# A tokenizer fed with host-laid patches in two halves of the batch, its global scores taken through the weights, and expert weights laid out by the host

## The chip, the cores and the metric

The kernel runs on one core of a Trainium2 chip. The metric is the device time of one execution in microseconds (us); the number compared is the median of several executions. One more execution is recorded by the hardware profiler, and all rows below come from it.

A core has five engines with an instruction stream each: TensorE (PE, matrix products into PSUM), VectorE (DVE), ScalarE (ACT), GpSimd (POOL) and SyncE (SP), which here issues nearly all loads and stores. They meet through semaphores. Transfers run on 16 DMA engines, whose mean busy share is the "DMA" of the profile.

## The reference, cut to what matters

A batch of 64 images and 77 text tokens of width C = 256 each go through three stages.

```python
# tokenizer: patches of 14x14x3 = 588 pixels, 6x6 of them used, as 2x2 windows of 3x3 patches
pe  = conv(x, conv_w, stride=14)
red = mean of pe over each window                       # (64, 4, C)
q   = ln(red) @ la_wq ; k, v = ln(window) @ la_wkv      # 1 query, 9 keys per window, 8 heads of 32
local_out = red + softmax(q k / 16) v @ la_proj_w + la_proj_b
gq  = ln(class_emb) @ ga_wq ; gk, gv = ln(local_out) @ ga_wkv   # 1 query, 4 keys per image
cls_out   = class_emb + softmax(gq gk / 16) gv @ ga_proj_w + ga_proj_b
patch_out = local_out @ mod_w + mod_b
h = concat([patch_out (4), cls_out (1), txt (77)])      # T = 82 tokens per image
# attention, 16 heads of 16, with a relative bias per head
h = h + softmax(q k * scale + bias) v @ w_out + b_out
# experts of low rank: 8 of them, two per token, for the first tokens of the list
h = h + sum over 2 experts of w_e * gelu(ln(h) @ w1A_e.T @ w1B_e) @ w2A_e.T @ w2B_e
```

The convolution has one set of weights for all patches. `gq` is the same for all images, because `class_emb` is.

## The kernel before

The program is three functions, one block each, with a barrier between them: `tokenizer_block` (from L55), `attention_block` (L637) and `expert_block` (L1080). The batch of 64 x 82 = 5248 tokens is 41 tiles of 128 rows. They stand in SBUF as `h_flat`; the tokenizer writes its five tokens per image to a list in memory (`fused_rows`), into which one long transfer (L148) has put the text, and the whole list is read back into `h_flat`.

**Tokenizer.** It works in 18 tiles of 128 patches: 64 images by the two windows `wi` of a column, for each `wj`, and for each of nine places (r, c) in the window. For a tile VectorE copies the pixels together (`copy_patch`, L404), TensorE turns them in five transposes (L253), ScalarE copies those to SBUF (L357, L359), and TensorE multiplies them with the turned convolution weights in five chunks, four of 128 pixels and one of 76 (`conv`, L227). VectorE copies the product (L499) and takes its statistics (L501). Then come 21 projections: the class query, and for each half `wj` one query and nine times keys and values, 512 wide. For each, VectorE normalises (`normalise`, L517), TensorE turns the rows (`xnT`, L269) and multiplies (`project`, L278), VectorE reads the product with a bias row (`consume`, L522). These loops are written out by hand and hold the order on each engine: on VectorE the normalise of item n stands ahead of the read of item n - 2. The gains of the layer norms are multiplied into the weights beforehand (L466), their offsets go through the weights as "shift rows" (L217). Window attention is VectorE's: products (L542), their sums (L545), softmax (L549 to L555), weighting (L558), sum over the keys (L562). The tails on TensorE: turn (L308), output projection (L317), patch output (L325), global keys and values (L335), turn and class projection (L340, L344). POOL takes the reciprocal roots (L185, L187) and scatters the slots of the experts' lists in 32 indirect transfers (L177).

**What SP's queue sets.** All loads are issued on SP in the order of the program: routing tables, identity, convolution weights, six transfers of images (L138), weights (L142), bias rows, the text (L148); after the last convolution `wqkv` (L150), after the patch outputs their four stores (L156), after the class token its store (L158), and when these have landed the four loads of `h_flat` (L162).

**Attention and experts.** At the start of its block SP issues `wout` (L709), the bias row, five tables (L712) and the expert weights (L713 to L716), then the stores of finished tiles (L721). VectorE's first instruction that needs the tables is at L1041. The expert block turns the first factors `w1a` and `w2a` with TensorE (L1186, L1192) and ScalarE copies (L1273, L1277), while the tokens of the first slots are gathered (L1143) and their statistics taken (L1335).

Of the kernel before, what the change touches and what calls it, by code (L numbers as in the profile page):

```python
# [14 lines left out]
C = 256  # L15
# [14 lines left out]
CHUNKS = [128, 128, 128, 128, PIX - 512]  # L30
# [14 lines left out]
def col(ap, n):  # L45

    return ap.rearrange("(c p) -> p c", p=128)


# [5 lines left out]
def tokenizer_block(nc, S, I, R, H, ident_all):  # L55

    NN = NTOK // 128 * TOPK
    with ExitStack() as ctx:
# [3 lines left out]
        img = sb("img", [128, CS, CIN, PS, IMG])  # L66

        early = R["early"]
        cw_nat = early[:, 0:2 * PIX].rearrange("p (t x) -> p t x", t=2)
        cwT = early[:, 2 * PIX:2 * PIX + 5 * C].rearrange("p (q c) -> p q c", q=5)  # L70
        patch = early[:, 2 * PIX + 5 * C:4 * PIX + 5 * C].rearrange("p (u x) -> p u x", u=2)
        patchT = early[:, 4 * PIX + 5 * C:].rearrange("p (u q t) -> p u q t", u=2, q=5)
        attn = R["attn"]
        wraw = attn["wraw"]
        pe = sb("pe", [128, WIN, NW, C])

        spare = img[:].rearrange("p r c y x -> p (r c y x)")
        kv = spare[:, 0:WIN * NW * 2 * C].rearrange("p (w n c) -> p w n c", w=WIN, n=NW)
        prod = spare[:, WIN * NW * 2 * C:WIN * NW * 2 * C + NW * C].rearrange("p (n c) -> p n c", n=NW)
        red = sb("red", [128, WIN, C])  # L80
        xn = sb("xn", [128, 2, C])
        xT = sb("xT", [128, 2, 2, 128])
        qv = sb("qv", [128, WIN, C])
# [3 lines left out]
        vec = sb("vec", [128, 8, 2])  # L87
        shiftb = sb("shiftb", [128, 4, 2, 128])
        bq_row = sb("bq_row", [128, C]); bkv_row = sb("bkv_row", [128, 2 * C])
        gbq_row = sb("gbq_row", [64, C]); gbkv_row = sb("gbkv_row", [64, 2 * C])  # L90
        pj_row = sb("pj_row", [128, C]); mod_row = sb("mod_row", [128, C]); gpj_row = sb("gpj_row", [64, C])
        cls = sb("cls", [64, C])
        NS = 20
        stats = sb("stats", [128, NS + 3, 6]); mv = sb("mv", [128, NS + 3, 2]); rs = sb("rs", [128, NS + 3])
        mhalf = sb("mhalf", [128, NS + 3])
        sc = sb("sc", [128, NW, H8]); sx = sb("sx", [128, H8]); ssum = sb("ssum", [128, H8]); rsum = sb("rsum", [128, H8])
        agg = sb("agg", [128, WIN, C]); aggT = sb("aggT", [128, 2, 2, 128])
# [25 lines left out]
        def _(sp):  # L123
# [29 lines left out]
            for wi in range(WIN):  # L153
                for wj in range(WIN):
                    t = wi * WIN + wj
                    sp.dma_start(fused[:, t, :], pout[64 * wi:64 * wi + 64, wj, :]).then_inc(S["tok_out"], 16)  # L156
# [1362 lines left out]
```

## Time and profile before

| | |
|---|---|
| median of three executions | 851.23 us (851.07 to 852.0) |
| the profiled execution | 855.09 us, span 853.3 us, 21494 instructions |
| TensorE busy | 688.8 us (81%), weight loads 529.1 us (62%) |
| VectorE, ScalarE, POOL busy | 551.9 us (65%), 394.6 us (46%), 287.4 us (34%) |
| mean granted clock of TensorE | 0.905 |

The time of an execution is the span plus what lies around it. TensorE's granted clock is written as a share of full speed: 1.00 is 2.4 GHz, 0.50 is 1.2 GHz. In a row of the timeline, the first number is the start in us from the span's start, the second the duration; then engine, line, operation, out<-in, the tile and how many instructions the row takes together; in brackets is how long the engine had stood idle and what released it. "SPq" is SP's queue of DMA issues; such a row tells of the issue, not of the transfer.

### The profile page before, as it was taken

The numbers are of one execution on the slowest core, as the hardware profiler recorded it, in microseconds if no ns is written. First come the engines' busy times: TensorE is split into PE (matmuls) and PEld (weight loads), VectorE is DVE, ScalarE is ACT, GpSimd is POOL, SyncE is SP. The second block draws the span as 40 slices with busy tenths as digits, with TensorE's granted clock in tenths as the row PEclk, the third lists the DMA queues.
The fourth block names the chain that finished last, engine by engine and source line by source line (L and its number), as shares of the span: only waits on it lengthen the run. The fifth ranks groups of instructions, "written<-read, shape, count | busy, mean of one in ns | idle before, by whom it ended". The sixth has DMA issues, their size and how long they took to land. (4 is left out here: it accounts for less than half of the span.)

```text
span 853.3 us, 21494 instructions
## 1 busy us (share of the span) xinstructions
PE 688.8 (81%) x8366; PEld 529.1 (62%) x8366; DVE 551.9 (65%) x1189; ACT 394.6 (46%) x931; POOL 287.4 (34%) x361
## 2 busy tenths in 40 slices
PE   1869696471469999999999999999987479999960
PEld 1657542320247777777778777777775468888850
DVE  0536658834448888888888888788772246666625
ACT  1111111000035676666666666667664335555533
POOL 2375200001282333334143323340001455767333
PEclk9979899775669999999999999999997679999985
DMA  8990100004920000000000000000000412222127
GB/s 153 218 324 12 37 1 0 1 12 152 317 39 8 15 15 15 15 18 17 14 15 15 14 15 15 15 21 14 15 15 19 99 58 68 82 70 75 52 72 268
DMA packets 34691, 51.20 MB, mean 60 GB/s; under 512 B 8960, under 2 KB 26208, under 8 KB 34464
## 3 DMA queue, kind: packets, MB, share of 16 engines
q1 hardware_dynamic: 29440, 39.55, 16.4%
q0 software_dynamic: 5152, 10.29, 4.2%
q8 instruction: 68, 1.11, 0.6%
q14 instruction: 31, 0.25, 0.1%
HBM read 36.89 MB, written 18.00 MB: 64 GB/s over the span
## 5 line engine op out<-in xcount | busy, mean ns | idle before, releaser
L1023 DVE TENSOR_REDUCE mx<-psS 82x8 f32<-82x656 f32 x128 | 106.3, 831 | 34.1 <-PE psS L825 34.1
L834 PE MATMUL psP<-ident_all,prob 82*82 82x82 f32 x1024 | 118.7, 239 | 9.3 <-ACT probT L960 9.3
L960 ACT ACTIVATE probT<-psP 82x328 f32<-82x328 f32 x256 | 112.4, 439 | 27.3 <-PE psP L834 27.3
L834 PEld LDWEIGHTS psP<-ident_all,prob 82*82 82x82 f32 x1024 | 91.1, 121 | 53.6 <-issue 30.1
L755 POOL TENSOR_TENSOR h_flat<-h_flat,po 128x256 f32<-128x256 f32 x41 | 29.8, 726 | 257.0 <-ACT po L947 257.0
L1025 DVE TENSOR_TENSOR prob<-psS,mx 82x656 f32<-82x656 f32 x128 | 107.0, 836 | 4.4
L952 ACT ACTIVATE prob<-prob 82x656 f32<-82x656 f32 x128 | 94.3, 738 | 0.0
L802 PE MATMUL psQ<-hT,early 128*128 128x328 f32 x256 | 85.5, 459 | 0.6 <-ACT hT L915 0.5
L812 PE MATMUL psQ<-early,hT 128*82 128x256 f32 x256 | 67.4, 387 | 0.1
L930 ACT ACTIVATE oT<-psO 128x328 f32<-128x328 f32 x64 | 28.4, 443 | 75.9 <-PE psO L846 75.9
L825 PE MATMUL psS<-kT,qT 32*82 32x82 f32 x2048 | 53.9, 243 | 10.4 <-DVE kT L1011 10.4
L825 PEld LDWEIGHTS psS<-kT,qT 32*82 32x82 f32 x2048 | 44.1, 150 | 18.2 <-DVE kT L1011 12.8
L802 PEld LDWEIGHTS psQ<-hT,early 128*128 128x128 f32 x256 | 44.9, 195 | 13.5 <-issue 1.9
L1295 ACT ACTIVATE f_hT<-psH 128x1024 f32<-128x1024 f32 x39 | 39.9, 1024 | 27.1 <-PE psH L1224 26.4
L742 POOL TENSOR_SCALAR xh<-h_flat,a_mv,a_rst 128x256 f32<-128x256 f32 x41 | 50.2, 1224 | 4.5
L846 PE MATMUL psO<-probT,vv 82*32 82x82 f32 x2048 | 50.1, 239 | 1.3 <-ACT attT L939 1.3
L1157 POOL DMA_INDIRECT entry_rows<-yv,slot_entry x39 | 39.9, 1022 | 29.0 <-ACT yv L1302 22.2
L1011 DVE SCALAR_TENSOR_TENSOR qT<-psQ,ownq,qadd 128x328 f32<-128x328 f32 x64 | 32.8, 555 | 25.4 <-PE psQ L802 25.3
L1224 PE MATMUL psH<-t1T,w1bs 64*128 64x128 f32 x624 | 47.6, 294 | 0.0
L227 PE MATMUL tk_ps<-early 128*128 128x256 f32 (+1 forms) x180 | 47.1, 415 | 0.0
L1236 PE MATMUL psT<-f_hT,w2as 128*64 128x128 f32 x624 | 43.5, 282 | 4.2 <-DVE t L1377 4.2
L1011 DVE SCALAR_TENSOR_TENSOR kT<-psQ,own,kadd 128x328 f32<-128x328 f32 x64 | 32.8, 555 | 20.3 <-PE psQ L802 20.3
(222 smaller groups left out, 1300.7 us busy)
## 6 DMA issues: line engine op xcount, KB each, us to landing
img<-in_x SPq DMA_DIRECT2D x6, 1008.0 KB, 20.6
out<-h_flat SPq DMA_DIRECT2D x41, 128.0 KB, 1.7
fused_rows<-in_txt SPq DMA_DIRECT2D x1, 4928.0 KB, 25.1
h_flat<-entry_rows SPq DMA_DIRECT2D x6, 512.0 KB, 6.3
h_flat<-fused_rows SPq DMA_DIRECT2D x1, 2176.0 KB, 16.6
ex_w2a<-in_ff_w_A SPq DMA_DIRECT2D x1, 2048.0 KB, 12.3
ex_w1b<-in_ff_w_B SPq DMA_DIRECT2D x2, 1024.0 KB, 17.2
out<-h_flat SPq DMA_DIRECT2D x8, 256.0 KB, 4.5
```

What stands on the lines that cost most here:

```text
L742: pool.tensor_scalar(xh[:, n % 3, :], H[:, n, :], mv[:, n % 4, 0:1], rst[:, n % 4:n % 4 + 1], ALU.subtract, ALU.mult).then_inc(S["xh_ready ...
L802: mm = te.matmul(bank(("qk", 4 * q + j))[:, 0:QT], wqkv[:, c, 128 * j:128 * j + 128], hT[:, c, a:a + QT], start=(c == 0), stop=(c == 1))
L812: mm = te.matmul(bank(("val", b))[0:T, 0:C], hT[:, c, a:a + T], wv[:, c, :], start=(c == 0), stop=(c == 1))
L825: mm = te.matmul(psS[0:T, g, s:s + T], qT[rows, par, a, t, cols], kT[rows, par, a, t, cols], start=True, stop=True)
L834: mm = te.transpose(psP[0:T, s * T:s * T + T], prob[:, b % 2, g, s, :], ident_all[0:T, 0:T])
L846: mm = te.matmul(psO[32 * k:32 * k + 32, s * T:s * T + T], vv[:, b % 4, h, :], probT[:, b % 2, h % 8 // 2, 2 * (h // 8) + h % 2, :], start ...
L952: act.activation(prob[:, b % 2, 2 * half:2 * half + 2, :, :], prob[:, b % 2, 2 * half:2 * half + 2, :, :], ACT.Exp).then_inc(S["prob_ready ...
L960: act.activation(probT[:, b % 2, g, :, :].rearrange("p s t -> p (s t)"), psP[0:T, 0:4 * T], ACT.Copy).then_inc(S["probT_ready"], 1)
L1011: ins = v.scalar_tensor_tensor(out=dst[:, q % 2, a, t, :].rearrange("p (b t) -> p b t", b=4), in0=bank(("qk", 4 * q + j))[:, 0:QT].rearran ...
L1023: v.tensor_reduce(mx[:, half, :, :], s4, X, ALU.max).then_inc(S["max_ready"], 1)
L1025: v.tensor_tensor(prob[:, b % 2, 2 * half:2 * half + 2, :, :], s4, mx[:, half, :, :].unsqueeze(3).to_broadcast([T, 2, 4, T]), ALU.subtract ...
L1224: mm = te.matmul(psH[:, j % 2, half, f * 128:f * 128 + 128], w1bs[rows, j % 2, f * 128:f * 128 + 128], t1T[rows, j % 2, :], start=True, st ...
```

## The change

- **Patches.** The host lays `x` out as `patches` (for each of 18 tiles, five chunks of 118 pixels by 128 columns, the last two rows of zeros) and the convolution weights as `conv_rows`. `PCH` is 118. `copy_patch`, the transposes and their copies go; patches come in five groups of 1, 3, 5, 4 and 5 tiles (`GROUPS`), issued between the other loads.
- **Two halves.** A tile now holds the four windows of 32 images. Tiles 0 to 8 are the first half, 9 to 17 the second. `items` is the order of the 22 projections. The second half's convolutions stand on TensorE behind the first half's projections, the first half's tail between them, and its tokens are stored, and the tiles 0 to 19 of `h_flat` loaded, ahead of the second half's.
- **Order.** On VectorE `consume(n)` now stands ahead of `normalise(n + 2)`, and the dot products are taken per key (`dots`), behind both. Values are read by ScalarE, the sum over the window, the residual and the list scatters (15 and 17) are POOL's. The shift rows of the global weights stand on TensorE behind projection 6.
- **Global scores through the weights.** The scores come from `wgs`, the global key weights times the class query, summed by head, so the global keys are not computed. The weighted values of the four windows are added by a product with the matrix `sel`.
- **Hand-over.** Tiles 20 to 40 of `h_flat` are loaded at the start of the attention block, once the second half's tokens have landed, ahead of its constants.
- **Experts.** `w1a` and `w2a` come turned from the host; their transposes and copies go, and a buffer `yg_hi` of its own holds what shared one. The rest of attention and experts is as before.

The diff, cut ("..." stands for what is left out):

```diff
+PCH = -(-PIX // 5)
+H_LOADS = ((0, 3), (3, 20), (20, 30), (30, 41))
...
+        items += [("kv", h, 0), ("kv", h, 1), ("q", h, 0)]
+        if h == 1:
+            items.append(("lg", 0, 0))
+        items += [("kv", h, k) for k in range(2, NW)]
+        if h == 0:
+            items.append(("gq", 0, 0))
+    items.append(("lg", 1, 0))
+    place = {item: n for n, item in enumerate(items)}
+    mv_order = [("gq", 0, 0)] + [("kv", 0, k) for k in range(NW)] + [("q", 0, 0)] + [("kv", 1, k) for k in range(NW - 1)]
...
+        patches = big[0:PCH, 0:18 * 5 * 128].rearrange("p (n q t) -> p n q t", n=18, q=5)
+        H = big[:, 0:NB * T // 128 * C].rearrange("p (n c) -> p n c", c=C)
+        cwT = sb("cwT", [PCH, 5, C])
...
-            sp.dma_start(cw_nat, I["conv_w"].rearrange("(t p) c y x -> p t (c y x)", p=128)).then_inc(S["conv_in"], 16)
-            for r in range(CS):
-                for wi in range(WIN):
-                    y0 = (wi * CS + r) * PS
-                    sp.dma_start(img[64 * wi:64 * wi + 64, r, :, :, :],
-                                 I["x"][:, :, y0:y0 + PS, :]).then_inc(S["img_in%d" % r], 16)
-            for name, tile in (("la_wq", wq), ("la_wkv", wkv), ("la_proj_w", wpj), ("ga_wq", gwq), ("ga_wkv", gwkv),
-                               ("ga_proj_w", gwpj), ("mod_w", wmod)):
-                sp.dma_start(tile[:], I[name].rearrange("(c p) n -> p c n", p=128)).then_inc(S["tk_w_in"], 16)
...
+            sp.dma_start(cwT[:], I["conv_rows"]).then_inc(S["conv_in"], 16)
+            for k, (lo, hi) in enumerate(GROUPS):
+                if k == 1:
+                    sp.dma_start(ident_all[:], I["ident"]).then_inc(S["ident_in"], 16)
+                    sp.dma_start(cols[:], I["cols"]).then_inc(S["ident_in"], 16)
+                    sp.dma_start(cls[:], row(I["class_emb"], 128)).then_inc(S["ident_in"], 16)
+                    sp.dma_start(entry[:], I["entry"]).then_inc(S["r_entry"], 16)
+                    sp.dma_start(R["list"], I["unfilled"]).then_inc(S["r_entry"], 16)
+                if k == 3:
+                    sp.dma_start(wq[:], I["la_wq"].rearrange("(c p) n -> p c n", p=128)).then_inc(S["law_in"], 16)
+                    sp.dma_start(wkv[:], I["la_wkv"].rearrange("(c p) n -> p c n", p=128)).then_inc(S["law_in"], 16)
+                sp.dma_start(patches[:, lo:hi, :, :], I["patches"][:, lo:hi, :, :]).then_inc(S["img_in%d" % k], 16)
+            sp.dma_start(gwq[:], I["ga_wq"].rearrange("(c p) n -> p c n", p=128)).then_inc(S["gaw_in"], 16)
+            sp.dma_start(gwkv[:], I["ga_wkv"].rearrange("(c p) n -> p c n", p=128)).then_inc(S["gaw_in"], 16)
+            for name, tile in (("la_proj_w", wpj), ("mod_w", wmod), ("ga_proj_w", gwpj)):
+                sp.dma_start(tile[:], I[name].rearrange("(c p) n -> p c n", p=128)).then_inc(S["prw_in"], 16)
...
+                for w in range(HW):
+                    sp.dma_start(fused[HB * h:HB * h + HB, w, :], pout[HB * w:HB * w + HB, h, :]).then_inc(S["tok_out%d" % h], 16)
+                sp.wait_ge(S["cout_ready"], h + 1)
+                sp.dma_start(fused[HB * h:HB * h + HB, HW, :], cout[:, h, :]).then_inc(S["tok_out%d" % h], 16)
+                if h == 0:
+                    sp.wait_ge(S["txt_in"], 16)
+                    sp.wait_ge(S["conv_done"], 18)
+                    sp.wait_ge(S["tok_out0"], 16 * 5)
+                    for k, (lo, hi) in enumerate(H_LOADS[:2]):
+                        sp.dma_start(H[:, lo:hi, :], R["fused"][128 * lo:128 * hi, :].rearrange("(n p) c -> p n c", p=128)).then_inc(S["h_in%d" % k], 16)
...
+            rstd(0)
+            for k in range(1, NW):
+                add_patch(0, k)
+                if k % 3 == 2:
+                    rstd(1 + k // 3)
...
+            pool.wait_ge(S["r_entry"], 32)
             pool.wait_ge(S["r_addr"], 1)
-            for n in range(NN):
-                pool.indirect_dma_start(out=slots, out_offset=bass.IndirectOffsetOnAxis(addri[:, n:n + 1], 0),
-                                        in_=entry[:, n:n + 1], in_offset=None).then_inc(S["r_listed"], 16)
+            list_entries(0, 15)
+            residual(0)
+            for k in range(1, NW):
+                add_patch(1, k)
+                if k == 2:
+                    rstd(5)
+                if k == 5:
+                    rstd(6)
+            rstd(7)
+            rstd(8)
+            rstd(9)
+            residual(1)
+            list_entries(15, NN)
...
-                te.wait_ge(S["patchT_ready"], 2 * (n + 1))
                 if n == 0:
-                    te.wait_ge(S["cwT_ready"], 5)
+                    te.wait_ge(S["conv_in"], 16)
+                for k, (lo, hi) in enumerate(GROUPS):
+                    if n == lo:
...
+                if n == 9:
+                    te.wait_ge(S["v_read"], NW)
+                for q in range(5):
+                    mm = te.matmul(PS8[n % 2][:, 0:C], patches[:, n, q, :], cwT[:, q, :], start=(q == 0), stop=(q == 4))
                 mm.then_inc(S["conv_done"], 1)
...
+            for n in range(6):
+                conv(n)
...
+            shift_rows(0, wq, slice(0, C), PS8[4][:, 0:C])
+            shift_rows(1, wkv, slice(0, 2 * C), PS8[5][:, :]).then_inc(S["shift_ps"], 1)
+            for n in range(6, 9):
+                conv(n)
+            xnT(0)
+            for n in range(10):
+                if n < 9:
+                    xnT(n + 1)
+                project(n)
+                if n == 6:
+                    te.wait_ge(S["gaw_in"], 32)
+                    te.wait_ge(S["shiftb_ready"], 4)
+                    te.wait_ge(S["shift_rows"], 2)
+                    shift_rows(2, gwq, slice(0, C), PS8[4][:, 0:C])
+                    shift_rows(3, gwkv, slice(C, 2 * C), PS8[4][:, C:2 * C]).then_inc(S["shift_ps"], 1)
+            for n in range(9, 16):
+                conv(n)
...
+            project(10)
+            conv(17)
+            xnT(11)
+            turn_lout(0)
...
+            def normalise(n):
+                kind, h, k = items[n]
...
+                v.tensor_scalar(xn[:, n % 2, :], src, mv[:, m, 0:1], rs[:, m:m + 1], ALU.subtract, ALU.mult).then_inc(S["xn_ready"], 1)
+            def consume(n):
+                kind, h, k = items[n]
...
+                v.wait_ge(S["proj_ps"], n + 1)
+                if kind == "kv":
+                    v.tensor_tensor(kv[:, k, 0:C], bank[:, 0:C], bkv_row[:, 0:C], ALU.add).then_inc(S["proj_read"], 1)
...
+            def dots(k):
+                chain(v.tensor_tensor(kv[:, k, 0:C], kv[:, k, 0:C], qv[:], ALU.mult))
+                chain(v.tensor_reduce(sc[:, k, :], kv[:, k, 0:C].rearrange("p (h d) -> p h d", h=H8), X, ALU.add))
...
+            for n in range(10):
+                consume(n)
+                if n + 2 < 10:
+                    normalise(n + 2)
+                if n >= 3:
+                    dots(n - 3)
+                if n == 8:
+                    v.wait_ge(S["shift_ps"], 2)
+                    v.tensor_copy(gbq_row[:], PS8[4][:, 0:C]).then_inc(S["shift_rows"], 1)
+                    v.tensor_copy(gbv_row[:], PS8[4][:, C:2 * C]).then_inc(S["shift_rows"], 1)
...
+            sp.wait_ge(S["tok_out1"], 16 * 5)
+            for k, (lo, hi) in list(enumerate(H_LOADS))[2:]:
+                sp.dma_start(H[:, lo:hi, :], A["fused"][128 * lo:128 * hi, :].rearrange("(n p) c -> p n c", p=128)).then_inc(S["h_in%d" % k], 16)
...
+def patch_rows(x):
+    s = CS * PS
+    a = np.asarray(x)[:, :, :WIN * s, :WIN * s].reshape(2, NB // 2, CIN, WIN, CS, PS, WIN, CS, PS)
+    a = a.transpose(2, 5, 8, 0, 4, 7, 3, 6, 1).reshape(PIX, 2 * NW, 128)
+    a = np.concatenate([a, np.zeros((5 * PCH - PIX, 2 * NW, 128), a.dtype)])
+    return a.reshape(5, PCH, 2 * NW, 128).transpose(1, 2, 0, 3)
```

SP's queue of loads before, from the tables on (names are out<-in with the shape):

```order
L131 DMA entry<-in_entry 128x32
L132 DMA slot_list<-in_unfilled 16x384
L133 DMA ident_all<-in_ident 128x128
L134 DMA early<-in_conv_w 128x2x588
L138 DMA img<-in_x 64x3x1344 x6
L142 DMA wq<-in_la_wq 128x2x256
L142 DMA wkv<-in_la_wkv 128x2x512
L142 DMA wpj<-in_la_proj_w 128x2x256
L142 DMA gwq<-in_ga_wq 128x2x256
L142 DMA gwkv<-in_ga_wkv 128x2x512
```

The same queue now (`big` is the tile that `patches` and `h_flat` share):

```order
L139 DMA cwT<-in_conv_rows 118x1280
L150 DMA big<-in_patches 118x640
L142 DMA ident_all<-in_ident 128x128
L143 DMA cols<-in_cols 128x26
L144 DMA cls<-in_class_emb 128x256
L145 DMA entry<-in_entry 128x32
L146 DMA slot_list<-in_unfilled 16x384
L150 DMA big<-in_patches 118x1920
L150 DMA big<-in_patches 118x3200
L148 DMA wq<-in_la_wq 128x2x256
L149 DMA wkv<-in_la_wkv 128x2x512
L150 DMA big<-in_patches 118x2560
```

Six image transfers into 64 partitions have become five into 118, with the weights between them; a last patch group and the global weights follow.

TensorE before, around the shift rows of the global keys and values (`tk_ps` is PSUM, `early` the turned patches and the convolution weights):

```order
L227 MATMUL tk_ps<-early 128x256 x5
L217 MATMUL tk_ps<-gwkv,shiftb 64x512 x2
L253 MATMUL tk_ps<-ident_all,early 128x128 x4
L253 MATMUL tk_ps<-ident_all,early 76x128
L227 MATMUL tk_ps<-early 128x256 x5
```

TensorE now, from projection 6 of the first half to its last:

```order
L289 MATMUL tk_ps<-wkv,xT 128x256 x2
L297 MATMUL tk_ps<-wkv,xT 128x256 x2
L257 MATMUL tk_ps<-gwq,shiftb 128x256 x2
L257 MATMUL tk_ps<-gwkv,shiftb 128x256 x2
L268 MATMUL tk_ps<-ident_all,xn 128x128 x2
L289 MATMUL tk_ps<-wkv,xT 128x256 x2
L297 MATMUL tk_ps<-wkv,xT 128x256 x2
L268 MATMUL tk_ps<-ident_all,xn 128x128 x2
L289 MATMUL tk_ps<-wkv,xT 128x256 x2
L297 MATMUL tk_ps<-wkv,xT 128x256 x2
```

The global shift rows have moved from between the convolutions to between the projections, and the convolutions L251 of the second half stand behind them.

VectorE before, in the projections of the first half (`img` holds the keys and values):

```order
L517 TENSOR_SCALAR xn<-pe,mv,rs 128x256
L522 TENSOR_TENSOR img<-tk_ps,bkv_row 128x512
L517 TENSOR_SCALAR xn<-pe,mv,rs 128x256
L522 TENSOR_TENSOR img<-tk_ps,bkv_row 128x512
L517 TENSOR_SCALAR xn<-pe,mv,rs 128x256
L522 TENSOR_TENSOR img<-tk_ps,bkv_row 128x512
```

VectorE now, in the same place:

```order
L611 TENSOR_TENSOR kv<-tk_ps,bkv_row 128x256
L603 TENSOR_SCALAR xn<-pe,mv,rs 128x256
L626 TENSOR_TENSOR kv<-kv,qv 128x256
L627 TENSOR_REDUCE sc<-kv 128x8
L611 TENSOR_TENSOR kv<-tk_ps,bkv_row 128x256
L603 TENSOR_SCALAR xn<-pe,mv,rs 128x256
```

The read of the keys has moved ahead of the next normalise, and the dot product of an earlier key follows both.

## Rows read from the trace of the kernel before

**Rows 1.** Waits of SP's queue: waited for, total, times, longest (us).
```profile
SPq L156 <- DVE pout L615: 82.0, 1, 82.0
SPq L150 <- PE tk_ps L227: 52.0, 1, 52.0
SPq L158 <- DVE pe L630: 20.5, 1, 20.5
```

**Rows 2.** Timeline, the hand-over to attention.
```profile
200.98 0.45 SPq L158 DMA_DIRECT2D fused_rows<-pe  x1
202.90 6.04 SPq L162 DMA_DIRECT2D h_flat<-fused_rows  x4
...
223.38 0.17 DVE L1041 TENSOR_SCALAR ownq<-own 128x2 f32<-128x2 f32 x1 [10.08 <-DMA own<-in_own]
...
241.61 1.43 PE L825 MATMUL psS<-kT,qT 32*82 32x82 f32 x32
```

**Rows 3.** Page, part 6, DMA issues: KB each, us from issue to landing.
```profile
img<-in_x SPq DMA_DIRECT2D x6, 1008.0 KB, 20.6
```

**Rows 4.** Windows: stretch, length, busy of PE, PEld, DVE, ACT, POOL, clock, DMA share, GB/s.
```profile
25.00:30.00 5.00, 4.45 (x13) 3.11 (x11) 4.47 (x13) 0.97 (x4) 0.00 (x0) 1.00 1.02 210
210.00:215.00 5.00, 0.00 (x0) 0.00 (x0) 3.20 (x7) 0.00 (x0) 3.78 (x6) 0.50 1.10 350
```

**Rows 5.** Timeline of the first 60 us: an SP issue, a list scatter, two convolutions' time.
```profile
5.25 0.44 SPq L131 DMA_DIRECT2D entry<-in_entry  x1
...
34.91 0.97 POOL L177 DMA_INDIRECT slot_list<-entry,addri  x1 [0.30 <-issue]
...
44.99 2.33 PE L227 MATMUL tk_ps<-early 128*128 128x256 f32 x10
...
55.52 4.33 PE L227 MATMUL tk_ps<-early 128*128 128x256 f32 x10
```

**Rows 6.** Timeline, window attention of the second half on VectorE.
```profile
157.15 2.55 DVE L545 TENSOR_REDUCE sc<-img 128x72 f32<-128x2304 f32 x1
...
161.67 2.56 DVE L558 TENSOR_TENSOR img<-img,sc 128x2304 f32<-128x2304 f32 x1
...
164.26 4.02 DVE L562 TENSOR_REDUCE agg<-img 128x256 f32<-128x2304 f32 x1
```

**Rows 7.** Timeline, projections and what VectorE does between them.
```profile
107.70 1.88 PE L278 MATMUL tk_ps<-wkv,xT 128*128 128x512 f32 x4
...
109.64 1.88 PE L278 MATMUL tk_ps<-wkv,xT 128*128 128x512 f32 x4
...
125.73 0.41 DVE L517 TENSOR_SCALAR xn<-pe,mv,rs 128x256 f32<-128x256 f32 x1
...
126.19 0.44 PE L269 MATMUL tk_ps<-ident_all,xn 128*128 128x128 f32 x2
126.20 0.42 DVE L522 TENSOR_TENSOR qv<-tk_ps,bq_row 128x256 f32<-128x256 f32 x1
```

**Rows 8.** Timeline, the tails: turn, POOL's roots, softmax, class projection.
```profile
168.34 0.69 PE L308 MATMUL tk_ps<-ident_all,agg 128*128 128x128 f32 x2 [10.09 <-DVE agg L562]
...
173.81 0.71 POOL L187 TENSOR_TENSOR rs<-rs,mhalf 128x2 f32<-128x2 f32 x1
...
192.46 0.17 DVE L549 TENSOR_SCALAR sc<-sc 64x32 f32<-64x32 f32 x1
...
197.24 0.47 PE L340 MATMUL tk_ps<-ident_all,pe 64*128 64x64 f32 x2 [8.10 <-DVE pe L562]
...
200.53 0.42 DVE L630 TENSOR_TENSOR pe<-pe,gpj_row 64x256 f32<-64x256 f32 x1
```

**Rows 9.** Timeline, the start of the expert block.
```profile
671.09 1.09 ACT L1277 ACTIVATE w2aT<-psH 128x512 f32<-128x512 f32 x2 [0.25 <-PE psH L1192]
...
674.21 1.40 DVE L1335 BATCH_NORM_STATS2 f_stats<-xin 128x6 f32<-128x256 f32 x4 [17.42 <-DMA xin<-out,slot_token]
```

**Rows 10.** Page, first line.
```profile
span 853.3 us, 21494 instructions
```

More of the change, by code:

```diff
@@ L116, in tokenizer_block, with gain, shift, stat_of @@
         slots = R["list"].rearrange("p j -> (p j)").rearrange("(n a) -> n a", a=1)
-        tiles = [(wj, r, c) for wj in range(WIN) for r in range(CS) for c in range(CS)]
+        fused = R["fused"].rearrange("(b t) c -> b t c", t=T)
+        def gain(k, c):
+            return cols[:, 4 * k + c:4 * k + c + 1]
+        def shift(k):
+            return cols[:, 4 * k + 2:4 * k + 4]
+        def stat_of(item):
+            kind, h, k = item
+            return {"kv": 10 * h + 1 + k, "q": 10 * h, "lg": 20 + h, "gq": 22}[kind]
         block = ctx.enter_context(nc.Block())
@@ new lines, in project @@
+                if kind == "kv":
+                    h = items[n][1]
+                    before = [m for m in range(n % 2, n, 2) if items[m][0] == "kv" and items[m][1] == h]
+                    if before:
+                        te.wait_ge(S["v_read"], v_count[items[before[-1]]])
+                    te.wait_ge(S["pe_ready"], 9 * h + 9)
+                    for c in range(2):
+                        mm = te.matmul(PS8[n % 2][:, 0:C], xT[:, n % 2, c, :], w[:, c, C:2 * C], start=(c == 0), stop=(c == 1))
@@ new lines, in _ @@
+            copy_pe(9)
+            copy_pe(10)
+            exponent(0)
+            for n in range(11, 16):
+                copy_pe(n)
+            copy_aggT(0)
+            copy_xT(10)
+            copy_pe(16)
+            copy_pe(17)
+            copy_xT(11)
+            copy_loutT(0)
+            for n in range(11, 22):
+                if n < 21:
+                    copy_xT(n + 1)
+                copy_v(n)
+                if n == 14:
+                    act.wait_ge(S["bias_ps"], 1)
+                    for c in range(2):
+                        ins = act.activation(wqkv[:, c, :], wqkv[:, c, :], ACT.Copy, scale=cols[:, 16 + c:17 + c])
+                    ins.then_inc(S["wqkv_scaled"], 1)
+                if n == 15:
+                    global_exponent(0)
+                if n == 19:
+                    copy_gaggT(0)
@@ L622, in _, with statistics @@
[L622 to L630 removed]
+            def statistics(item, src):
+                k = stat_of(item)
+                chain(v.bn_stats(stats[:, k, :], src))
+                v.bn_aggr(mv[:, k, :], stats[:, k, :]).then_inc(S["mv_ready"], 1)
@@ new lines, in _ @@
+            v.wait_ge(S["shift_rows"], 2)
+            normalise(0)
+            normalise(1)
+            mean_patch(0)
+            for n in range(10):
+                consume(n)
[7 more added lines that the diff above has]
+                    v.tensor_copy(gbv_row[:], PS8[4][:, C:2 * C]).then_inc(S["shift_rows"], 1)
```

820 lines of the change are left out of this document (403 added, 417 removed).

## The prediction, made before the changed kernel had run

> **What bounds the kernel now.** I read the waits of the DMA queue first, then the timeline of the first 250 us, then busy time by windows. The program runs as three blocks with a barrier between them: tokenizer, attention, experts. The diff rewrites the first, hands attention its inputs differently, and drops one preparation from the third. SP's queue shows the skeleton of the tokenizer [rows 1]: 52.0 us until the last convolution, 82.0 until the patch tokens, 20.5 until the class token. It is one chain with nothing beside it: images, convolutions, projections, window attention, residual, patch token, class attention; the last DMA of tokens goes out at 200.98, all hidden rows are read back from 202.90 on, and attention's first real work waits until 223.38 for constants queued behind that read-back; the first scores start at 241.61 [rows 2]. Attention from there on is the same code, so I carry it over unchanged: the change is worth what it moves the moment of 223.38.
>
> **What a load costs.** The images come as six transfers into 64 partitions each [rows 3] and run with all engines busy at 210 GB/s; the read-back into 128 partitions runs at 350 [rows 4]. Divided by 16 engines that is 13.1 and 21.9 GB/s each, and into 64 partitions 26.3 GB/s for every eight of them. The Trainium skill (SBUF — State Buffer, the section on the DMA port swizzle) says that 64 partitions reach 8 of the 16 ports, at some 27 GB/s a port; the trace's 210 against 350 agrees.
>
> The new loads have 118 rows: the 588 pixels of a patch as five chunks of 118 instead of four of 128 and one of 76. All transfers of this trace have a first dimension that 16 divides (64, 128 or 16 rows), so it shows only even splits over 16 engines. If the split has to be even, 118 = 2 x 59 leaves two engines. That is my forecast's assumption, and I give it most of the chance because every transfer here, read by its GB/s, is shared evenly. The Trainium skill says it outright (DMA: Bandwidth & Descriptors, "Why a DMA increments its semaphore by 16 and not by 1"): the number of engines is the largest one up to 16 that divides the slowest dimension of both sides, 100 partitions giving 10 and 127 giving 1. No run here shows an uneven case, and by that rule the forecast stands.
>
> Each of the two engines then moves 59 rows of 5,120 bytes of convolution weights and 18 patches x 2,560 bytes: 59 x 51,200 = 3.02 MB. All other loads use all engines and queue behind on these two; up to the global query and key weights that adds a sixteenth of 1.5 MB, with small things 0.12 MB, so 3.14 MB each. The sixth issue of SP's queue begins at 5.25 [rows 5], data flow from about 7 and the last receipt takes 1. How fast one engine goes alone no row shows. From below: 21.9 GB/s, what each gets when 16 share the memory (13.1 as the extreme, the image rate). I take 26.3, the rate per eight partitions, as an engine that writes row after row should find no wider door than such a group. So the global weights land at t: 3.14 MB / 26.3 GB/s = 119 us after the start at 8, t = 127 us (at 21.9 GB/s: 151). The skill's page on DMA gives 27 GiB/s per engine; by that, an estimate, t would be 116.
>
> **Where that bites.** TensorE runs the first half of the batch (convolutions 0 to 8, then ten projections). Its sixth to ninth patch arrives with the third group, (0.302 MB of weights + 0.151 + 0.453 + 0.755 of patches)/26.3 = 63 us of transfer, so at about 71; three and more convolutions at 2.33 (4.33 at half clock) [rows 5], shift rows and seven projections take it to 71 + 16 + 22 = 109. Then it stands before the shift rows of the global weights, in order, until 127: projections 7 to 9, the second half's convolutions and all the rest are queued behind. Both patch groups of the second half have landed by then.
>
> **From t to the class token.** Five pieces, with durations of before:
> 1. Four shift matmuls at half clock, 4.33 / 5 = 0.87 each: 3.5, and three projections of 3.06 (piece 3): 12.7.
> 2. Nine convolutions x 2.33 = 21, with the transposes, output projection and class query between them 2.5: 23.5. VectorE's softmax and sums of the first half (2.56 + 4.02 and small ones) [rows 6] lie beside.
> 3. Eleven projections. Before, one began every 1.94 (107.70, 109.64): the next normalise was issued ahead of the read of the last projection. Now it stands behind it on VectorE, and TensorE's next transposes wait for it: 1.88 of matmuls + 0.27 from the transposes' start to the next projection's, + read 0.42 + normalise 0.41 [rows 7], and 0.08 for the handovers = 3.06. Nine of these are 27.5; query and global item 3.3; patch output and the 14 bias matmuls 3.8: 34.6. The dot products, 0.9 each, now fit in VectorE's gaps instead of 2.56 for the products and 2.55 for their sums at the end.
> 4. Last read, two dot products, softmax, weighting 2.56, sum 4.02, shift row 0.42: 11.3.
> 5. The global tail, at half clock as before [rows 8]: from the turn at 168.34 to the rstd on POOL, done at 174.52, 6.2; normalise 0.4; the patch output and transposes ahead of it on TensorE 2.5; projection with scores 2.6; softmax as 192.46 to 194.02, 1.6; weighting on a fourth of the numbers 0.6; class projection from its turn at 197.24 to the last sum at 200.95, 3.7: 17.6.
> Sum 99.7, say 100, so the class token is ready at 227 (before at 200.95).
>
> **Hand-over.** Only tiles 20 to 40 are still to be read: 2.75 MB with 0.65 MB of constants behind it. Before it was 5.25 + 0.65 MB in 20.5 us (202.90 to 223.38) [rows 2], of which 16.9 at 350 GB/s; now 9.7 + 3.6 = 13.3, and 2.6 until the last store has landed: 16 where it was 22.4. The constants arrive at 243, against 223.4: **+20 us**.
>
> **What I cost at nothing.** POOL's 32 list scatters (0.97 and 0.30 between them, so 1.27) [rows 5] move, 15 behind the first half's patch sums and 17 behind the second mean; both lie in TensorE's stretches, 22 us against some 45 to the next thing asked of POOL. Without that cover the last rstd would be late by what is left. Patch copies, transposes (five per patch) and their ACT copies go, 18 x 0.6 us of TensorE; they would count were TensorE not waiting for data. Expert weights: eight turns end at 672.2, but VectorE starts at 674.21 on the gathered tokens [rows 9], so their removal gains nothing; 0.5 MB more is loaded beside attention.
>
> The sum is made against the profiled execution, 855.09 us (span 853.3) [rows 10]; the median of the runs is 851.23, 3.9 lower. A difference carries over, so 851.2 + 20 = **871 us**.
>
> **The rivals.**
> *The 118 rows are spread over all engines.* For it: loads of both widths kept all 16 engines busy, and nothing in the trace refuses an uneven split. Then 6.04 MB need 17 us at 350 GB/s, TensorE is never short of data: index matmuls to 11, six convolutions to 27, shift rows, three more to 36, seven projections of 3.06 to 60. From there 100 less 3 for a warm clock, and 16: 173 instead of 223.4, so 801 us. Its chance is 0.17.
> *One engine alone is faster than eight partitions' share.* At 29 GB/s t is 116 and the time 860; at 32 and above the constants arrive no later than 223.4 and nothing is lost. It decides the sign from 32 GB/s on. Chance 0.06; against it, the fastest stretch read here gives an engine 21.9 [rows 4].
> *An engine alone gets its image rate, 13.1 GB/s,* because latency per row and not the port is its limit: t = 248, the time 992. Chance 0.02: in the read-back an engine does 21.9 with rows of 1 KB.
>
> **How the numbers follow.** Forecast (two engines at 21.9 to 28 GB/s) 0.75. Its own range is 864 to 895; with 7 us of doubt on the five pieces, 857 to 902. Taken down to 846, for the second rival, the range leaves out the first and the third and little else, 0.2 in all. 0.2%, 1.7 us, is what a measurement can tell. Faster by more: the first rival whole, half the second and a little of the forecast, 0.22. Within: 0.03. Slower: 0.75.
>
> **What would show it.** In the profile after: the DMA share in the first 120 us near 2/16 instead of full, GB/s near 50; time to landing of the patch groups 20 to 40 us each; TensorE idle of some 18 us at the shift rows of the global weights, released by a DMA; projection spacing 3.1; class token 100 after that; a_w constants 16 later. It is wrong if the DMA share is full for the first 20 us (then 801), or if the projections run at 2 us, which would give back up to 10, or if attention's batches take another time than now.

## The result, and the profile after

The changed kernel takes 877.62 us (median of 4, 876.2 to 878.3), the kernel before 851.62: 26 us slower. The ratio on record is 1.0289 (95% interval 1.0264 to 1.0314); the two medians divide to 1.0305, inside that interval. Forecast were 871 us, 20 slower, with a range of 846 to 902.

The page of the changed kernel, its span, granted clock, DMA share and GB/s in 40 slices:

```profile
span 876.5 us, 21431 instructions
PEclk9767969977567999999999999999998579999995
DMA  2111327003290000000000000000000312222117
GB/s 56 62 74 54 101 89 255 8 1 122 71 319 15 8 14 15 21 14 14 15 20 14 15 15 20 15 14 14 15 21 13 84 56 73 68 89 73 48 58 278
```

A slice is 21.9 us. For the first 130 us the DMA share is one to three tenths, where images before ran on all engines [rows 4]. A stretch in which only patches move, TensorE standing still, by windows (columns as in [rows 4]):

```profile
60.00:70.00 10.00, 0.00 (x0) 0.00 (x0) 0.00 (x0) 0.00 (x0) 0.00 (x0) 0.50 0.12 52
```

0.12 of 16 engines is two, and 52 GB/s are 26 each. The trace also holds every update of the semaphore that a transfer counts up as it lands. The third patch group gives three: one at 23.3, as soon as it is issued, and two as its data lands, at 72.2 and 72.9. The two loads of global weights have 128 rows and give 32: 28 of them between 93.1 and 101.9, the last four between 127.5 and 131.0. So 14 engines had delivered their part of these weights 29 us before the two that were still busy with patches.

TensorE's longest waits (waited for, total, times, longest):

```profile
PE tk_ps L251 <- DMA big<-in_patches: 49.4, 3, 19.4
PE tk_ps L257 <- DMA gwkv<-in_ga_wkv: 19.9, 1, 19.9
PE psX L1334 <- DVE f_xn L1470: 17.4, 2, 16.3
PE tk_ps L268 <- DVE xn L603: 16.5, 16, 1.5
PE psO L920 <- DMA own<-in_own: 14.8, 1, 14.8
```

Patches are waited for three times, then the global weights, once, for 19.9 us. The wait for `xn` now stands behind nearly every read, 16 times; in the kernel before, TensorE waited for `xn` six times, 14.3 us together, 6.9 of it the first time. The timeline, in the order of the prediction's steps (the row of SP is the issue of `gwq`, described at the end):

```profile
71.35 19.78 SPq L151 DMA_DIRECT2D gwq<-in_ga_wq  x1
72.98 6.54 PE L251 MATMUL tk_ps<-cwT,big 118*128 118x256 f32 x20 [19.44 <-DMA big<-in_patches]
...
131.08 2.08 PE L257 MATMUL tk_ps<-gwq,shiftb 128*128 128x256 f32 x4 [19.92 <-DMA gwkv<-in_ga_wkv]
...
142.43 15.35 PE L251 MATMUL tk_ps<-cwT,big 118*128 118x256 f32 x70 [0.56 <-ACT kv L444]
...
165.80 0.44 PE L268 MATMUL tk_ps<-ident_all,xn 128*128 128x128 f32 x2 [1.10 <-DVE xn L603]
...
172.01 2.84 PE L399 MATMUL tk_ps<-cols,wqkv 128*128 128x1 f32 x24
...
203.34 1.03 PE L297 MATMUL tk_ps<-wkv,xT 128*128 128x256 f32 x4
...
215.78 0.69 PE L308 MATMUL tk_ps<-ident_all,agg 128*128 128x128 f32 x2 [11.41 <-DVE agg L649]
...
233.69 0.41 DVE L680 TENSOR_TENSOR cout<-tk_ps,cls_row 32x256 f32<-32x256 f32 x1 [3.38 <-PE tk_ps L352]
234.13 0.30 SPq L166 DMA_DIRECT2D fused_rows<-cout  x1
...
248.33 0.17 DVE L1186 TENSOR_SCALAR ownq<-own 128x2 f32<-128x2 f32 x1 [9.84 <-DMA own<-in_own]
...
268.94 1.42 PE L970 MATMUL psS<-kT,qT 32*82 32x82 f32 x32
...
697.57 1.41 DVE L1458 BATCH_NORM_STATS2 f_stats<-xin 128x6 f32<-128x256 f32 x4 [16.32 <-DMA xin<-out,slot_token]
```

The constants arrive at 248.33 instead of 223.38 [rows 2], 25.0 later; the experts start at 697.57 instead of 674.21 [rows 9], 23.4 later; the span ends 23.2 later. The loss arises before attention. The medians differ by 26.0, more than the spans, because the profiled execution of before (855.09) lies 3.5 above the median of its runs and that of after (878.3) only 0.7.

### The profile page after: what moved, and what is told of

It reads as the page before. It is cut to its first block and busy times, and to the rows that moved or that the text cites. A ratio compares the mean times of both kernels' runs of the same rounds, so it can differ in the third digit from the quotient of the medians.

```text
span 876.5 us, 21431 instructions
## 1 busy us (share of the span) xinstructions
PE 667.2 (76%) x8314; PEld 526.6 (60%) x8314; DVE 526.5 (60%) x1182; ACT 391.6 (45%) x926; POOL 296.0 (34%) x382
## 5 line engine op out<-in xcount | busy, mean ns | idle before, releaser
L900 POOL TENSOR_TENSOR big<-big,po 128x256 f32<-128x256 f32 x41 | 29.8, 726 | 257.0 <-ACT po L1092 257.0
L947 PE MATMUL psQ<-hT,wqkv 128*128 128x328 f32 x256 | 86.8, 465 | 0.5 <-ACT hT L1060 0.5
L251 PE MATMUL tk_ps<-cwT,big 118*128 118x256 f32 x180 | 46.6, 422 | 50.0 <-DMA big<-in_patches 49.4
L251 PEld LDWEIGHTS tk_ps<-cwT,big 118*128 118x128 f32 x180 | 38.2, 215 | 58.5 <-DMA big<-in_patches 34.3
L957 PE MATMUL psQ<-wqkv,hT 128*82 128x256 f32 x256 | 66.7, 383 | 0.1
L970 PEld LDWEIGHTS psS<-kT,qT 32*82 32x82 f32 x2048 | 43.8, 149 | 18.3 <-DVE kT L1156 12.8
L947 PEld LDWEIGHTS psQ<-hT,wqkv 128*128 128x128 f32 x256 | 45.9, 199 | 14.1 <-issue 2.8
L887 POOL TENSOR_SCALAR xh<-big,a_mv,a_rst 128x256 f32<-128x256 f32 x41 | 50.2, 1224 | 4.5
L427 ACT ACTIVATE pe<-tk_ps 128x256 f32<-128x256 f32 x18 | 6.9, 383 | 97.4 <-PE tk_ps L251 97.4
## 6 DMA issues: line engine op xcount, KB each, us to landing
ex_w2aT<-in_w2aT SPq DMA_DIRECT2D x1, 2048.0 KB, 12.4
```

The costliest lines, as they stand in the source:

```text
L251: mm = te.matmul(PS8[n % 2][:, 0:C], patches[:, n, q, :], cwT[:, q, :], start=(q == 0), stop=(q == 4))
L887: pool.tensor_scalar(xh[:, n % 3, :], H[:, n, :], mv[:, n % 4, 0:1], rst[:, n % 4:n % 4 + 1], ALU.subtract, ALU.mult).then_inc(S["xh_ready ...
L947: mm = te.matmul(bank(("qk", 4 * q + j))[:, 0:QT], wqkv[:, c, 128 * j:128 * j + 128], hT[:, c, a:a + QT], start=(c == 0), stop=(c == 1))
L957: mm = te.matmul(bank(("val", b))[0:T, 0:C], hT[:, c, a:a + T], wv[:, c, :], start=(c == 0), stop=(c == 1))
L970: mm = te.matmul(psS[0:T, g, s:s + T], qT[rows, par, a, t, cols], kT[rows, par, a, t, cols], start=True, stop=True)
```

## The experiments

The engines of a transfer, first. One edit, four numbers; each adds rows of zeros to the patches and the convolution weights, with the same instructions:

```diff
-PCH = -(-PIX // 5)
+PCH = 128          # also 120, 124, 127
```

> The changed kernel with 128 rows in place of 118 for patches and convolution weights (the rest zeros, 6.55 MB instead of 6.04). My theory (a transfer is shared only by as many engines, up to 16, as divide its rows): all 16 engines work, the patches land within about 20 us, TensorE finds no data missing, the constants of attention arrive near 175 us instead of 248.3, the time is 800 to 806 us. Rival (the slow loading comes from something else, as the form of the source in memory or loads that stand between the patches): the DMA share stays near 2/16 and the time at 870 to 885 us.

> 120 rows. My theory (largest divisor up to 16): 15 engines, DMA share near 0.9 while the patches load, time 800 to 807 us as with 128 rows. Rival (only multiples of 16, or powers of two, are spread; all else goes on 2 engines): near 877 us.

> 124 rows = 4 x 31. My theory: 4 engines, DMA share 4/16, some 104 GB/s; each moves 1.71 MB until the global weights have landed, at about 8 + 65 = 73 us, as TensorE finishes its seventh projection near 77; the time is then 820 to 830 us. Rival (2 engines for all that 16 does not divide): near 877 us. Rival (rows shared out unevenly, the slow 118 having another cause): near 803.

> 127 rows, a prime. My theory: one engine, DMA share 1/16, 26 GB/s; it moves 6.6 MB until the global weights have landed at about 8 + 252 = 260 us, 129 us later than with 118 rows; the time is near 1006 us. If one engine alone is faster than each of two were together (29 GB/s), 980 us. Rival (2 engines): near 885.

These four ran on a chip on which the kernel before took 902.2 us (median of 7), so differences and ratios count, not the times. On it TensorE also stood before transposes of `xn` (L268) without a releaser ("issue", 11.4 us in the tokenizer with 128 rows, 6.9 with 120, 5.6 with 127); neither the changed kernel's trace nor that of 128 rows on another chip shows it.

| rows | engines by the divisor | time | ratio to before | moved to the 851.6 of the other chips |
|---|---|---|---|---|
| 128 | 16 | 849.5 us | 0.9411 (0.9348 to 0.9475) | 801 us |
| 120 | 15 | 850.4 us | 0.943, one execution | 803 us |
| 124 | 4 | 876.9 us | 0.972, one execution | 828 us |
| 118 | 2 | 877.6 us | 1.0289, another chip | 877.6 us |
| 127 | 1 | 1045.1 us | 1.158, one execution | 986 us |

Windows of the four kernels in the same stretches; with 128 rows and with 120:

```profile
20.00:30.00 10.00, 10.00 (x44) 8.04 (x44) 3.18 (x12) 2.40 (x7) 5.99 (x10) 1.00 1.02 396
```

```profile
20.00:30.00 10.00, 9.33 (x44) 7.89 (x43) 2.90 (x11) 1.74 (x5) 4.41 (x8) 1.00 1.01 241
```

With 124 and with 127:

```profile
60.00:70.00 10.00, 7.41 (x29) 5.24 (x28) 4.04 (x12) 1.86 (x5) 6.03 (x9) 0.79 0.25 98
```

```profile
60.00:70.00 10.00, 0.00 (x0) 0.00 (x0) 0.00 (x0) 0.00 (x0) 0.00 (x0) 0.50 0.06 26
```

0.25 is four engines and 0.06 one; 98 and 26 GB/s are 24.5 and 26 each. With 120 rows the share is 1.01 where 0.9 was expected, so it doesn't tell 15 engines from 16. The updates of the semaphore do. The third patch group has one early update and then as many as engines deliver: 2 with 118 rows, 15 with 120, 4 with 124, 1 with 127; with 128 rows all 16 come together (17.2 to 19.3 us).

The order of the times is that of the largest divisor and not of the bytes: 127 rows are fewer than 128 and cost 196 us more. That shows the forecast's assumption. The rivals of two engines for every count that 16 does not divide fall with 120 and 124. The time of 127 rows, moved by the ratio, is 986 and lies nearer to the 980 of a faster lone engine than to 1006, but the ratio also shrinks a wait for data, and one engine moves 26 GB/s on this chip as each of two does on the other. In the trace the global weights release TensorE at 261.37, where 260 was expected, 130 after the 131.08 of 118 rows. From there to attention's constants (389.62) it is 128.3 us, 11 more than the 117.3 of 118 rows, which I put down to the slower chip. The constants were expected near 175 with 128 rows; on this chip they came at 189.90.

The same 118 rows without padding, in two transfers (the waits for them count to 32 in place of 16), and 128 rows once more:

```diff
-            sp.dma_start(cwT[:], I["conv_rows"]).then_inc(S["conv_in"], 16)
+            for a, b in ((0, 112), (112, PCH)):
+                sp.dma_start(cwT[a:b, :, :], I["conv_rows"][a:b, :, :]).then_inc(S["conv_in"], 16)
...
+                for a, b in ((0, 112), (112, PCH)):
+                    sp.dma_start(patches[a:b, lo:hi, :, :], I["patches"][a:b, lo:hi, :, :]).then_inc(S["img_in%d" % k], 16)
```

> The changed kernel with its 118 rows, each of its six transfers cut in two, of rows 0 to 111 and 112 to 117. My theory (112 = 16 x 7, so all 16 engines; 6 rows go on 6): DMA share full in the first 20 us, the same time as with 128 rows within 3 us, a ratio of 0.938 to 0.944. Rival (it is the 118 in the tile, its 5,120 and 2,560 byte rows or its place in memory, and not the rows of one transfer): the ratio stays at 1.029.

> The kernel of 128 rows once more, beside split112 and on a chip that is not the first one if it falls so. By the first ratio, 0.941, and the time of the kernel before: 801 us where the kernel before takes 851. If the first chip's idle of TensorE between instructions in the tokenizer was part of the ratio, a ratio of 0.935 to 0.94.

split112: 806.93 us, ratio 0.9455 (0.9418 to 0.9491). rows128_again: 804.53 us, 0.9448 (0.9405 to 0.9491); the kernel before took 852.76 beside both. The tile, its rows and its data are those of the changed kernel, and 71 us go with the cut alone: it is the number of rows of one transfer. Its semaphores agree: the pair of transfers of the third patch group gives 23 updates, 16 for 112 rows and 1 + 6 for the six. With 128 rows the constants come at 170.07 on this chip (175 expected). The ratio of 128 rows is somewhat above the first one, within its interval, and not at the 0.935 to 0.94 that were expected if the first chip's idle was part of it.

Then the order of the loads in the starved queue, with 118 rows:

```diff
                 if k == 3:
                     sp.dma_start(wq[:], ...)
                     sp.dma_start(wkv[:], ...)
+                    sp.dma_start(gwq[:], I["ga_wq"].rearrange("(c p) n -> p c n", p=128)).then_inc(S["gaw_in"], 16)
+                    sp.dma_start(gwkv[:], I["ga_wkv"].rearrange("(c p) n -> p c n", p=128)).then_inc(S["gaw_in"], 16)
                 sp.dma_start(patches[:, lo:hi, :, :], I["patches"][:, lo:hi, :, :]).then_inc(S["img_in%d" % k], 16)
-            sp.dma_start(gwq[:], I["ga_wq"].rearrange("(c p) n -> p c n", p=128)).then_inc(S["gaw_in"], 16)
-            sp.dma_start(gwkv[:], I["ga_wkv"].rearrange("(c p) n -> p c n", p=128)).then_inc(S["gaw_in"], 16)
```

> The changed kernel with 118 rows, its two loads of global weights moved ahead of the two patch groups of the second half. My theory (TensorE stands at the shift rows of the global weights for 19.9 us because they queue behind patches that it needs only later): they land near 76 us, the wait goes, the second half's convolutions begin 18 us earlier, at 124 instead of 142, with their patches there by then; 18 us less than the changed kernel, a ratio near 1.009. Rival (the starved queue only shows up as a wait for the last patches): the ratio stays at 1.02 to 1.03.

862.25 us, ratio 1.0103 (1.0082 to 1.0123) beside a kernel before of 852.61, against 1.0289: some 16 us of the 26 come back (15.4 by the medians), where 18 were expected. TensorE's waits have lost that for `gwkv`, and hold the three for patches as before:

```profile
PE tk_ps L251 <- DMA big<-in_patches: 50.4, 3, 20.8
```

The second half's convolutions begin at 125.28 (124 expected), and attention's constants come 16.9 us earlier than in the changed kernel:

```profile
231.47 0.17 DVE L1186 TENSOR_SCALAR ownq<-own 128x2 f32<-128x2 f32 x1 [10.00 <-DMA own<-in_own]
```

This shows the step "where that bites": the 19.9 us of waiting at the global shift rows were on the path.

Then VectorE's order in the projections, with 128 rows:

```diff
-                consume(n)
                 if n + 2 < 10:
                     normalise(n + 2)
+                consume(n)
```

(and the same in the second half's loop).

> The kernel of 128 rows, with VectorE's normalise(n + 2) ahead of consume(n) again in both projection loops. My theory (TensorE waits for the normalise behind the read, 3.2 us from projection to projection): the spacing falls to about 1.95, some 16 to 18 projections gain 1.2 each, 20 us less than with 128 rows alone, a ratio to the kernel before near 0.918. Rival (VectorE, whose work per item is 0.42 + 0.41 + 0.9, or POOL's roots take over as the wait): 5 to 10 us less, a ratio of 0.93 to 0.935.

788.89 us, ratio 0.9232 (0.918 to 0.9284). That is 15.6 us less than with 128 rows again by the medians, and 18 by the ratios, but the two were taken on different chips and their intervals leave room for 13 to 24. The two traces differ by less: the class token goes out 9.4 us earlier (146.56 instead of 155.95) and the span is 10.6 shorter. TensorE's wait for `xn`, with 128 rows and in norm_first:

```profile
PE tk_ps L268 <- DVE xn L603: 16.5, 16, 1.5
```

```profile
PE tk_ps L268 <- DVE xn L603: 4.1, 4, 1.5
```

The spacing, before this edit in the changed kernel and after it (128 rows):

```profile
102.87 1.03 PE L289 MATMUL tk_ps<-wkv,xT 128*128 128x256 f32 x4
...
106.07 1.03 PE L289 MATMUL tk_ps<-wkv,xT 128*128 128x256 f32 x4
```

```profile
45.65 1.03 PE L289 MATMUL tk_ps<-wkv,xT 128*128 128x256 f32 x4
47.60 1.03 PE L289 MATMUL tk_ps<-wkv,xT 128*128 128x256 f32 x4
...
51.71 1.03 PE L289 MATMUL tk_ps<-wkv,xT 128*128 128x256 f32 x4
```

3.20 becomes 1.95 in the first half. In the second half's loop, which also holds the tail of the first, it is in part longer (2.25 from 103.64 to 105.89 in the trace of norm_first). So the mechanism is shown by the wait that goes, 12.4 us of it. Its worth lies between 10 and 18 us: the ratio speaks for the theory's 20, the traces for the rival's 5 to 10.

The hand-over, both ways, and both on norm_first. In rows_late the early loads of hidden rows are moved behind the last tokens:

```diff
                     sp.wait_ge(S["tok_out0"], 16 * 5)
-                    for k, (lo, hi) in enumerate(H_LOADS[:2]):
-                        sp.dma_start(H[:, lo:hi, :], ...)
...
             sp.wait_ge(S["tok_out1"], 16 * 5)
-            for k, (lo, hi) in list(enumerate(H_LOADS))[2:]:
+            for k, (lo, hi) in enumerate(H_LOADS):
```

In tables_first attention's constants are moved ahead of the wait and of the hidden rows:

```diff
-            sp.wait_ge(S["tok_out1"], 16 * 5)
-            for k, (lo, hi) in list(enumerate(H_LOADS))[2:]:
-                sp.dma_start(H[:, lo:hi, :], ...)
             sp.dma_start(wout[:], ...)
...
+            sp.wait_ge(S["tok_out1"], 16 * 5)
+            for k, (lo, hi) in list(enumerate(H_LOADS))[2:]:
+                sp.dma_start(H[:, lo:hi, :], ...)
```

> norm_first with the two early loads of hidden rows moved behind the second half's tokens, so all 5.25 MB stand ahead of attention's constants, as before the change. My theory (the hand-over's term: 2.5 MB less to read after the last token, at 350 GB/s): the constants come 7.2 us later, ratio 0.923 + 0.0085 = 0.931 to 0.932. Rival (attention waits for its first tiles or for POOL's normalising, and not for these constants): 0.922 to 0.926.

> norm_first, and in attention's block the eight loads of constants (0.65 MB) ahead of the wait for the second half's tokens and of the 2.75 MB of hidden rows. My theory (the constants release attention's first products, and stand behind the rows): they arrive some 8 us earlier, the first products then wait for the third normalised tile, so 6 us less than norm_first, a ratio near 0.911. Rival (the hidden rows are needed as early, or the gain is lost at the start of attention): within 2 us of norm_first.

rows_late: 798.88 us, ratio 0.9366 (0.9334 to 0.9398). The class token goes out at 145.90 and the constants are there at 167.49, 21.6 later; in norm_first 146.56 and 160.69, 14.1. So 7.5 us, where 7.2 was worked out. The 20 tiles are 2.62 MB and not the 2.5 of the prediction; with these it is 7.5 at 350 GB/s. The median is 10 above that of norm_first, on another chip. In the traces attention's first scores come 7.3 later and the experts' first statistics 10.5, so some 3 us more are lost inside attention; their cause stays open.

```profile
167.49 0.17 DVE L1184 TENSOR_SCALAR ownq<-own 128x2 f32<-128x2 f32 x1 [15.12 <-DMA own<-in_own]
```

```profile
160.69 0.17 DVE L1186 TENSOR_SCALAR ownq<-own 128x2 f32<-128x2 f32 x1 [9.76 <-DMA own<-in_own]
```

tables_first: 781.11 us, ratio 0.9137 (0.9103 to 0.9172), 7.8 us less than norm_first. The constants are there at 151.33:

```profile
151.33 0.17 DVE L1186 TENSOR_SCALAR ownq<-own 128x2 f32<-128x2 f32 x1 [1.37 <-DMA own<-in_own]
```

9.4 us earlier, 1.0 of it because the class token went out earlier. Attention's first scores get 8.1 of it (172.76 instead of 180.83); I had expected 6.

> tables_first with 118 rows, cut in two as in split112. My theory: no difference to tables_first but 0.5 MB less to load, ratio 0.910 to 0.914. Rival (twelve issues instead of six, at 0.45 us each on SP, delay the first patches, and 6 engines carry more): 2 to 4 us more, 0.916 to 0.919.

best_split: 783.29 us, ratio 0.9189 (0.9157 to 0.9222). The ratio lies where the rival had put it (0.916 to 0.919) and above the theory's 0.910 to 0.914. But the two intervals overlap, the medians are 2 us apart and come from two chips, and the trace of best_split has the constants 2.4 us earlier (148.95) and the span 1.3 shorter. So whether the cut costs anything stays undecided. By its median tables_first is the fastest kernel here, 71 us under the kernel before.

Last, one part of the change alone: `w1a` and `w2a` turned by the host in the kernel before.

```diff
-            for n in range(2):
-                for q in range(NE // 2):
-                    mm = te.transpose(psH[:, 1, n, q * 128:q * 128 + 128], w1a[:, q, n * 128:n * 128 + 128], ident_all[:])
...
+            sp.dma_start(W["w1aT"][:], I["w1aT"]).then_inc(S["f_w1a_in"], 16)
+            sp.dma_start(W["w2aT"][:], I["w2aT"]).then_inc(S["f_w2a_in"], 16)
```

> The kernel before with only the expert weights laid out by the host and a buffer of its own for the gathered rows. My theory (the turns lie beside the gather of the first tokens): no change, ratio 0.998 to 1.001. Rival (the turns, or the power that they take, delay the first expert tile): 3 to 6 us less, ratio 0.993 to 0.996.

851.8 us, ratio 0.9981 (0.996 to 1.0003): no difference clear of noise, and at most 3.4 us by the interval. Its first expert statistics still wait for the gathered tokens:

```profile
670.84 1.40 DVE L1316 BATCH_NORM_STATS2 f_stats<-xin 128x6 f32<-128x256 f32 x4 [16.45 <-DMA xin<-out,slot_token]
```

## Why the prediction was right, point by point

The time, 877.6, lies 7 us above the forecast and within its range. The steps add up: 131.1 until the global weights (forecast 127), 103.0 to the class token (100), 14.2 for the hand-over (16) give the 248.3 of the constants (243).

**Two engines, and their rate.** Shown, by the DMA share of 0.12, by the updates of the semaphores, by the five row counts, and by the cut into 112 and 6. The rate was an estimate from eight partitions' share [rows 4], 26.3 GB/s; measured are 26. The reason given for it, that an engine should find no wider door than eight partitions, was not tested, so the closeness of the number may be luck. The Trainium skill's rule (DMA: Bandwidth & Descriptors, "Why a DMA increments its semaphore by 16 and not by 1"), the largest divisor up to 16, agrees with the traces: 2, 15, 4 and 1 engines delivered with 118, 120, 124 and 127 rows. The same page of the Trainium skill ("Specifications") gives about 27 GiB/s per engine, which is 29 GB/s; the measurement is lower, the lone engine of 127 rows did 26.

**Where it bites.** The third patch group was forecast at 71 (72.98), the end of the seventh projection at 109 (the trace has TensorE idle from 111.16), the global weights at 127 (131.08). Of the 4 us that t was short, the rate of 26.0 for 26.3 explains some 1.4; the rest wasn't looked for. The prediction let the sixth patch be the first to wait for the third group; it is the fifth, as `GROUPS` has one and three tiles ahead of it. That changes little, because TensorE's stretch from there to the first projection took 17.1 us where 16 was taken. global_early shows that the wait for the weights was on the path.

**From t to the class token,** forecast 100, measured 103.0. The rows above cut it into the five pieces: 131.08 to 142.43, 11.4 (12.7); to 165.80, 23.4 (23.5); to the end of the last projection at 204.4, 38.6 (34.6); to 215.78, 11.4 (11.3); to 234.10, 18.3 (17.6). The 1.94 between projections of before, from which the prediction starts, holds for its first half only; in its second half TensorE waited for `xn` there too, five times, and those projections began 2.9 to 4.9 apart. The term that was mis-sized is the third: a projection took 3.2 and not 3.06, and TensorE's granted clock fell in the middle of it,

```profile
165.00:185.00 20.00, 15.81 (x76) 11.94 (x77) 8.39 (x27) 4.57 (x10) 15.66 (x21) 0.77 0.04 8
```

where I had counted the half level (1.2 GHz) only for the ends. Before it fell, TensorE had run 24 short products of one column each (L399, row above) beside waits for `xn`. That they are the cause is not shown: no run leaves them out, and in the kernel before the clock also fell behind waits for `xn` alone:

```profile
144.63 3.34 PE L278 MATMUL tk_ps<-wkv,xT 128*128 128x512 f32 x4
```

The same product takes 1.88 at full clock [rows 7]. norm_first shows that the order of normalise and read is a cost, of 10 to 18 us in all.

**Hand-over.** Forecast 16, measured 14.2 (234.10 to 248.33). rows_late shows its term, 7.5 against 7.2.

**Costed at nothing.** The expert weights: experts_alone agrees, within 3.4 us. The list scatters: no wait for them stands among TensorE's; nothing was run on it. The removed patch copies and transposes: not separated; how much of the gain with 128 rows, where TensorE is not short of data, is theirs stays open. The same holds for the two halves and the global scores through the weights.

**Attention carried over.** This holds in sum, in part by luck. From the constants to the first scores it is 20.6 us and was 18.2 [rows 2], so the scores come 27.3 later and not 25.0. In the 12 us from 250 on TensorE's granted clock is 0.67, where it was 0.92 from 225 to 237 before, and the first products with the projection weights (L947, a row of 16) take 7.29 us instead of 5.03 (L802 before). From there to the experts 4.0 us come back, for which no cause was looked for, and 23.4 are left.

**The first rival's price** was 801 us for patches on all engines. rows128_again took 804.5 and split112 806.9, so the sum of what remains of the change was judged within 1%. With a row count that 16 divides the change brings 48 us; with 118 rows it costs 26.

## What to carry to other kernels

Before a layout is chosen for its arithmetic, look at what the row count of the transfer divides into: padding 118 rows to 128, or cutting it into 112 and 6, was worth 71 to 73 us of 878 with no other edit. 120 and 124 rows, on 15 and 4 engines, cost 1 and 27 us more than 128 here, in one execution each. In a profile, read the DMA share where a load is waited for: a low share beside a long wait was here a transfer on few engines, and all that queued behind it on those engines was late too; putting ahead of it what is needed first gave back 16 us. In a software pipeline on two engines, try the producer of the next item ahead of the reader of the last; here it took away 12.4 of 16.5 us of waiting.

## What was not expected of the hardware

With 120 rows the DMA share was as full as with 128 (1.01 and 1.02), but 241 GB/s moved instead of 396. With the cut into 112 and 6 it was the same:

```profile
20.00:30.00 10.00, 9.70 (x42) 7.64 (x42) 3.28 (x12) 1.54 (x4) 5.65 (x10) 1.00 1.07 237
```

Busy engines thus did some 15 to 16 GB/s each, against 25 with 128 rows. In these 10 us a packet of 12,800 bytes took 0.98 us with 120 rows and 0.93 with 112 and 6, against 0.48 with 128 (medians). TensorE's waits for patches stay small, 3.2 and 1.6 us against 0.5 and 0.7 with 128 rows on the same chips, though in the traces the constants come 5.3 and 4.7 us later; the times differ by 1 and 2.4 us, within the noise. The cause was not looked for.

An issue on SP can itself last while the engines are behind: that of `gwq` in the changed kernel took 19.78 us (71.35 to 91.13, row above), where with 128 rows it took 0.44 (11.92), and the bias rows were issued only at 125.61.
